# Stack places set one by one, half of a lookup level moved to ScalarE for three chunks, orders rewritten

## The reference

```python
x = _layernorm(x + _L0_attn_ref(x, Wq, Wk, Wv, Wo))      # softmax(q k^T / sqrt(dh)) v, times Wo
x = _layernorm(x + _L0_ffn_ref(x, gate_w, up_w, down_w, gate_scale, up_scale, down_scale))
x = _layernorm(x + _L1_attn_ref(x, wq, wk, wv, wo))
w = lut[idx]                                             # in _ghost_linear, for gate, up and down
x = _layernorm(x + _L1_ffn_ref(x, lut, gate_idx, up_idx, down_idx))
```

## Time and profile before

| | us |
|---|---|
| median of 3 runs | 352.78 (351.83 to 353.12) |
| profiled execution, its time | 352.02 |
| its span, first to last instruction | 350.2 |
| TensorE busy | 296.1 (85%) |
| VectorE busy | 254.2 (73%) |
| ScalarE busy | 221.5 (63%) |
| GpSimd busy | 213.6 (61%) |

### The profile page before, as it was taken

How to read it: one execution, slowest core, us unless ns; L and a number is a source line. 1 busy time by engine, 2 the same in 40 slices (tenths; PEclk the granted TensorE clock), 3 DMA queues, 4 the chain that set the end, 5 groups by cost and what they waited for, 6 DMA issues and landing times.

```text
span 350.2 us, 7093 instructions
## 1 busy us (share of the span) xinstructions
PE 296.1 (85%) x2608; PEld 206.3 (59%) x2608; DVE 254.2 (73%) x405; ACT 221.5 (63%) x408; POOL 213.6 (61%) x297
## 2 busy tenths in 40 slices
PE   8314667765777788999999999999999999999993
PEld 7202332222344354676766676687779788789993
DVE  7478978678689899999997696667664756325354
ACT  2333566677686776787686896698566656564440
POOL 5947255555573677869689755754565332766745
PEclk9955565696698999999999999999999999999998
DMA  6443351026300204500042123023506000100001
GB/s 189 125 106 118 92 154 46 2 71 168 100 0 2 63 17 123 161 4 2 3 130 65 33 65 100 2 72 94 180 22 187 7 3 1 34 2 31 2 2 60
DMA packets 24889, 23.07 MB, mean 66 GB/s; under 512 B 3558, under 2 KB 24854, under 8 KB 24854
## 3 DMA queue, kind: packets, MB, share of 16 engines
q1 hardware_dynamic: 24854, 22.61, 22.7%
HBM read 10.47 MB, written 3.26 MB: 39 GB/s over the span
## 4 chain that ended last, share of the span: by engine, by line
PE 68%; DVE 17%; issue 4%; ACT 3%; SPq 3%; POOL 2%; DMA 2%; POOLq 0%; DVEq 0%; ACTq 0%
PE FB L1259 15%; PE PV L1202 11%; PE MM L1147 9%; PE FB L1284 7%; DVE MX L955 7%; DVE LV L1065 5%; PE SC L1176 5%; PE FB L1101 4%; PE SC L1181 4%; PE FB L1231 3%; ACT PB L855 2%; PE FB L1121 2%; PE FB L1214 2%; POOL LV L739 2%; PE FB L1126 2%
## 5 line engine op out<-in xcount | busy, mean ns | idle before, releaser
L955 DVE TENSOR_REDUCE MX<-MM 128x4 f32<-128x1024 f32 x96 | 117.1, 1220 | 41.1 <-PE MM L1147 40.5
L855 ACT ACTIVATE PB<-SC 128x1024 f32<-128x1024 f32 x96 | 98.1, 1021 | 33.7 <-PE SC L1176 23.6
L1147 PE MATMUL MM<-KS,QS 62*128 62x256 bf16 (+1 forms) x384 | 48.6, 300 | 33.4 <-DVE MX L955 23.5
L721 POOL TENSOR_TENSOR HL<-HF,HH 128x256 fp32r<-128x256 f32 (+1 forms) x48 | 36.5, 769 | 36.6 <-ACT HH L832 36.5
L739 POOL TENSOR_SCALAR LV<-LB,LD,LT 128x432 f32<-128x432 uint8 x80 | 55.1, 709 | 2.0 <-DVE LB L1051 1.9
L1202 PE MATMUL PV<-PB,VP 128*32 128x256 f32 x768 | 55.4, 417 | 0.0
L1147 PEld LDWEIGHTS MM<-KS,QS 62*128 62x128 bf16 (+1 forms) x384 | 20.4, 99 | 57.0 <-DVE MX L955 35.0
L1065 DVE COPY_PREDICATED LV<-LB,LV 128x1728 f32<-128x1728 uint8 (+2 forms) x30 | 39.7, 1323 | 5.7 <-POOL LV L739 5.3
L1259 PE MATMUL FB<-XH,W 128*128 128x256 f32 x192 | 43.0, 305 | 0.0
L1259 PE MATMUL FB<-XL,W 128*128 128x256 f32 x192 | 38.5, 282 | 0.0
L1023 DVE SCALAR_TENSOR_TENSOR AA<-TH,FB 128x256 f32<-128x256 f32 (+1 forms) x48 | 19.9, 415 | 24.6 <-ACT TH L846 17.8
(11 more groups left out here) (107 smaller groups left out, 551.9 us busy)
## 6 DMA issues: line engine op xcount, KB each, us to landing
QS<-QP SPq DMA_DIRECT2D x48, 128.0 KB, 2.4
IX<-in_idx SPq DMA_DIRECT2D x10, 216.0 KB, 3.8
dw<-LO SPq DMA_DIRECT2D x10, 216.0 KB, 2.3
W1L<-dw SPq DMA_DIRECT2D x10, 216.0 KB, 3.3
KS<-KP SPq DMA_DIRECT2D x24, 64.0 KB, 2.0
XT<-in_xt SPq DMA_DIRECT2D x4, 256.0 KB, 3.2
X<-in_x SPq DMA_DIRECT2D x4, 256.0 KB, 3.2
RAW<-in_gate SPq DMA_DIRECT2D x4, 192.0 KB, 2.7
```

The lines of the kernel that those rows point to most:

```text
L721: pool.tensor_tensor(HL[0:r, i, :], HF[0:r, c % 2, :], HH[0:r, i, :].bitcast(F32), ALU.subtract).then_inc(h_parts, 1)
L855: act.activation(PB[:, quad % PB_QUADS, kt, :, :], SC[:, :, :], ACT.Exp, scale=DH[layer(j)] ** -0.5).then_inc(exp_done, 1)
L955: dve.tensor_reduce(mx, MM[:, :, :].rearrange("p (f i) s -> p f i s", f=2), axis=AX.X, op=ALU.max).then_inc(max_red, 1)
L1147: ins = pe.matmul(MM[:, 2 * f + i, :], QS[lo:lo + r, j % NST, qs + h, qt * P:(qt + 1) * P], keys(j)[lo:lo + r, j % NST, ks, :], start=True ...
```

## The change

Set-up: VectorE builds KONE first and then sets place after place: a clear of QS's place, and KS's place written from KONE in one instruction, without a clear of its own; each place raises `stacks_set` by one, and a stack copy of job j below 3 waits for j + 1. The clears of BITS and MS and the copy IDB stand between and behind the places. The value tile VP1 is cleared in a step `ones.4` of GpSimd's list, its first.

Lookup: for chunks 0, 1 and 2 the steps `lut1.c.2` and `lut1.c.3` are ScalarE's, with its activation Identity (scale and bias one value for each partition); `lut2.c` waits for both counts. The lists of all five engines are new.

```diff
+LUT_ACT = (0, 1, 2)
...
     "ACT": (
-        "q.0 kv.0 qmid.0 kmid.0 lutix.0 lutix.1 q.1 lutlow.0 q8.0 q8.1 q8.2 kv.1 qmid.1 q8.3 lutix.2 lutlow.1 q8.4 "
+        "lutix.0 q8.0 q.0 kv.0 kmid.0 qmid.0 lut1.0.2 lut1.0.3 kv.1 lutlow.0 lutix.1 lut1.1.2 lut1.1.3 q.1 q8.1 q8.2 "
...
+        def pool_parts(c):
+
+            return 4 * c - 2 * sum(i < c for i in LUT_ACT)
+
...
-                    sp.wait_ge(stacks_set, 1)
-                    if j >= NST:
+                    if j < NST:
+                        sp.wait_ge(stacks_set, j + 1)
+                    else:
...
-            link(pool.memset(VP1[:, :, :, :, :], 0.0))
-            pool.memset(VP1[:, :, :, :, 16:17], 1.0).then_inc(ones_pool, 1)
-
             for step in order("POOL"):
                 kind = step[0]
-                if kind in ("q", "kv"):
+                if kind == "ones":
+
+                    link(pool.memset(VP1[:, :, :, :, :], 0.0))
+                    pool.memset(VP1[:, :, :, :, 16:17], 1.0).then_inc(ones_pool, 1)
+                elif kind in ("q", "kv"):
...
+                elif kind == "lut1":
+
+                    _, c, part = step
+                    if c == LUT_ACT[0] and part == 2:
+                        act.wait_ge(lut_steps, 1)
+                    act.wait_ge(bit_done, c + 1)
+                    if c >= 1:
+                        act.wait_ge(low_done, c)
+                    for i in range(2 * part, 2 * part + 2):
+                        ins = act.activation(LV[:, i, :], LB[:, 0, :], ACT.Identity, scale=LD[:, i:i + 1],
+                                             bias=LT[:, 2 * i:2 * i + 1])
+                    ins.then_inc(level1_act, 1)
...
-            dve.memset(QS[:, :, :, :], 0.0)
-            link(dve.memset(KS[:, :, 0:4, :], 0.0))
+            mrow = IDN[:, :].rearrange("p (f r) -> p f r", f=2)[:, :, STACK[0]:STACK[0] + 2]
+
+            def set_place(i):
+
+                dve.memset(QS[:, i, :, :], 0.0)
+                dve.tensor_scalar(KS[:, i, 0:4, :], KONE[:, :].rearrange("p (o s) -> p o s", o=1).broadcast_to((P, 4, S)),
+                                  1.0, None, ALU.mult).then_inc(stacks_set, 1)
+
             link(dve.memset(KONE[:, :], 0.0))
+            dve.wait_ge(const_pool, 1)
+            link(dve.tensor_reduce(MROW[:, :], mrow, axis=AX.XY, op=ALU.add))
+            link(dve.tensor_scalar(KONE[:, :], KONE[:, :], MROW[:, 0:1], None, ALU.add))
+            set_place(0)
             for k in range(4):
-                ins = dve.memset(BITS[:, k:k + 1], 0x01010101 << k)
...
+                dve.memset(BITS[:, k:k + 1], 0x01010101 << k)
+            set_place(1)
+            dve.memset(MS[:, :, :], 0.0)
+            set_place(2)
+            link(dve.tensor_scalar(IDB[:, :], IDN[:, :], 1.0, None, ALU.mult))
...
-                        dve.wait_ge(level1, 4 * (c + 1))
+                        dve.wait_ge(level1, pool_parts(c + 1))
+                        if c in LUT_ACT:
+                            dve.wait_ge(level1_act, 2 * LUT_ACT.index(c) + 2)
```

More of the change, by code:

```diff
@@ L431, in two_layer_kernel @@
         level1 = sem("level1")
+        level1_act = sem("level1_act")
         lut_done = sem("lut_done")
@@ L909, in link @@
                 dve.wait_ge(dve_own, own[0])
-            dve.memset(QS[:, :, :, :], 0.0)
-            link(dve.memset(KS[:, :, 0:4, :], 0.0))
+            mrow = IDN[:, :].rearrange("p (f r) -> p f r", f=2)[:, :, STACK[0]:STACK[0] + 2]
[3 more added lines that the diff above has]
+                                  1.0, None, ALU.mult).then_inc(stacks_set, 1)
             link(dve.memset(KONE[:, :], 0.0))
+            dve.wait_ge(const_pool, 1)
+            link(dve.tensor_reduce(MROW[:, :], mrow, axis=AX.XY, op=ALU.add))
+            link(dve.tensor_scalar(KONE[:, :], KONE[:, :], MROW[:, 0:1], None, ALU.add))
+            set_place(0)
             for k in range(4):
-                ins = dve.memset(BITS[:, k:k + 1], 0x01010101 << k)
-            link(ins)
-            link(dve.memset(MS[:, :, :], 0.0))
-            dve.wait_ge(const_pool, 1)
-            mrow = IDN[:, :].rearrange("p (f r) -> p f r", f=2)[:, :, STACK[0]:STACK[0] + 2]
-            link(dve.tensor_reduce(MROW[:, :], mrow, axis=AX.XY, op=ALU.add))
-            dve.tensor_scalar(IDB[:, :], IDN[:, :], 1.0, None, ALU.mult)
-            link(dve.tensor_scalar(KONE[:, :], KONE[:, :], MROW[:, 0:1], None, ALU.add))
-            dve.tensor_scalar(KS[:, :, 0:4, :], KS[:, :, 0:4, :], MROW[:, 0:1], None, ALU.add).then_inc(stacks_set, 1)
+                dve.memset(BITS[:, k:k + 1], 0x01010101 << k)
[3 more added lines that the diff above has]
+            link(dve.tensor_scalar(IDB[:, :], IDN[:, :], 1.0, None, ALU.mult))
             def layer_norm(b, step):
```

## The result

| | before | changed |
|---|---|---|
| median | 352.95 (351.83 to 353.63, 4 runs) | 340.85 (339.58 to 342.28, 4 runs) |
| ratio, 95% interval | | 0.966 [0.961, 0.972] |
| profiled execution, its time and span | 352.02, 350.2 | 342.28, 340.4 |
| VectorE waits for row-max matmuls, row max 0 to 41 | 16.5, 20 times | 8.2, 15 times |

The account below looks back on a forecast made before the run. The prediction took VectorE to bound the kernel first and TensorE after. Start 2.6, GpSimd's relief 0.7, job 0's order zero and job 7 0.8 summed to 4.1 us, taking 352.78 to 348.7, range 347.0 to 351.0.

Parts of the forecast that it names:

- neighbours swapped: Lists of jobs 1 to 5: the other reorderings only swap neighbours while TensorE is full, so they gain nothing.

Follow-up runs that it names:

- lut_later: The changed kernel with level one of chunks 0 to 2 all on GpSimd and VectorE's lookups of chunks 1 and 2 placed later; 347.85 us, ratio 0.987.
- ve_before1: The changed kernel with VectorE's list of jobs 0 and 1 as it was before, the other four lists new; 353.43 us, ratio 1.004.

## What to carry to other kernels

Where two engines hand one buffer back and forth, list every wait above the usual hand-over, with the granted clock beside it, and sum them: the sum shows the size of what order and clock together hold (8.3 us here), and "neighbours swapped" is no reason for zero while such waits stand. Price a list of one engine against the list of its partner: the same three scores ahead of max.0.13 cost VectorE no wait in the changed kernel, 1.65 us in lut_later and 3.08 in ve_before1, by whether it has a lookup of its own beside them. Moving work to a third engine can be worth far more than its time, if it makes that partner's work ready at the place where it covers something.
